# Fourteen scan states fed by TensorE diagonals, scan outputs added by accumulating transposes, filled phase ends and split values in a four-layer kernel

## The chip, the cores and the metric

The kernel runs on one core of one Trainium2 chip. The metric is the device time of one launch in microseconds (us). Each engine has a queue of instructions of its own and waits for others on semaphores: TensorE (PE) multiplies and transposes, VectorE (DVE), ScalarE (ACT) and GpSimd (POOL) work on elements, SyncE (SP) issues transfers.

## The reference

x has 1024 tokens (4 sequences of 256) of 512 values, all fp32. Four layers follow, each between two norms:

```
x = x + ln(ssm(ln(x)))          # D_IN 1024, 16 states
x = x + ln(int_ffn(ln(x)))      # 1376 hidden, integer weights, scales per row
x = x + ln(attention(ln(x)))    # 32 query heads, 8 key/value heads, causal
x = x + ln(diff_ffn(ln(x)))     # 1792 hidden
# ssm: dt, B, C from x; for each channel d and state n, over time:
state = state * exp(dt * A) + dt * u * B ;  y = sum_n(state * C) ;  y = (y + x*D) * silu(gate)
# diff_ffn weights: base + mean(|w - base|) * sign(w - base)
```

## The kernel before

The program is a row of phases, each a block in which every engine has its own written-out order: `in` (projection), prologue, `scan`, `fa` (finish), `mi` (widen), `fb`, key and value, attention, `fd`. Nothing schedules at run time but semaphores; a phase's instructions don't start before the phase ahead has ended on all engines. Precise products split both operands in a high and a low part in fp32r: high*high, high*low and low*high, three matmuls. ACT makes the high part, DVE or POOL the low one.

**Scan** (`scan_phase`, L680). A tile is 128 channels of one sequence: 32 tiles, two to a turn of a loop (r = 0, 1). Its 16 states stand as 8 pairs of 2 x 256 columns. Of a pair the decay exp(dt*A) comes from ACT (L861); the inflow dt*u*B comes from POOL for 8 states (L798) and from PE for the other 8, as fp32 matmuls with a diagonal matrix that holds B (L1045, two for a pair). DVE scans each pair (L952, L958). The outputs are weighed with C by DVE for 8 states (L968) and by POOL for 8 (L810). PE adds the 16 weighed states and x*D into y by 17 fp32 matmuls of 256 columns with the identity (L1051, L1077). An fp32 matmul leaves two records in the trace. Two transposes a tile (L1036) turn dt*u for ACT, which makes the diagonals.

**Finish** (`finish_phase`, L160) multiplies the gated y, or the hidden values, with the down weights for 8 tiles of 128 tokens, normalizes, adds to x, normalizes again and transposes the result (L227) into the operands xh, xl of the next phase. **Widen** (`widen_phase`, L460) goes through F steps; a step is 48 matmuls of 512 columns (L538): 2 halves of the weights, 4 blocks of depth, 3 products, 2 halves of the tokens (h). For `mi` it also loads w and base of the last layer (L516), POOL subtracts them (L622) and ACT sums |w - base| (L563), which waits for nobody else in the step. Weights of step f are split by ACT (`prepare`, L558) and DVE (L634). Key and value (L1207) have the same form with steps of half the width.

**Attention** (`attention_mlp_phase`, L1317) makes 32 steps (8 groups g of 4 heads, 4 sequences b). In a step PE does the output products of the step behind it (24 matmuls, L1462 to L1464), transposes the probabilities (L1471, L1476), multiplies them with the values by 3 fp32 matmuls of 512 columns (`attend`, L1480 to L1484), the scores of the next step (L1448, L1450) and its queries (48 matmuls of 256 columns, L1437). DVE takes the maxima (L1817), scales the probabilities (L1828); POOL makes the low parts of the group's weights, wql (L1728) and wol (L1732), and the sine part of the rotation (L1724).

## Time and profile before

The median of 3 runs is 1802.15 us (1801.33 to 1806.17). The profiled execution took 1799.71 us; its span, from the first to the last instruction recorded, is 1797.9 us at a mean granted clock of 0.976.

| engine | busy us | share of the span | instructions |
|---|---|---|---|
| PE (matmuls, transposes) | 1671.7 | 93% | 8214 |
| PEld (weight loads, beside PE) | 1374.2 | 76% | 8214 |
| DVE | 1101.3 | 61% | 1608 |
| ACT | 867.7 | 48% | 1773 |
| POOL | 812.4 | 45% | 414 |

Busy time is an average over phases with different limits, so it is read by phase: the views of windows give it for a stretch, the timeline gives the start of each group of like instructions. A timeline's second column reaches to the modelled end of the last one and overlaps the next; a pace is read from one start to the next start.

### The profile page before, as it was taken

To read this page: it belongs to the slowest core of one execution; us is meant where nothing else is said; L and a number is where in the kernel's file an instruction comes from. 1 tells how busy PE (TensorE), PEld (TensorE's weight loads), DVE (VectorE), ACT (ScalarE), POOL (GpSimd) and SP (SyncE) were. 2 spreads that over 40 slices of the span, in tenths; PEclk is the share of its full clock that TensorE was granted. 3 is DMA by queue.
4 is the path that set the end of the run, shared out by engine and by line. 5 is a ranking of instruction groups with operands and counts; after the bars stand their busy time and mean duration, and the time that the engine had idled before them with its cause. 6 is when DMAs were issued, how large, how long until landed. Compare 5 with 4: busy or idle time off the path is not lost. (4 is left out here: it accounts for less than half of the span.)

```text
span 1797.9 us, 24221 instructions
## 1 busy us (share of the span) xinstructions
PE 1671.7 (93%) x8214; PEld 1374.2 (76%) x8214; DVE 1101.3 (61%) x1608; ACT 867.7 (48%) x1773; POOL 812.4 (45%) x414
## 2 busy tenths in 40 slices
PE   5995999999998799997998999999999999899998
PEld 4862788888886588786876888788787878788877
DVE  4337999999995433352915566665656667755422
ACT  2337777777763354233624454545444445543321
POOL 2212999999994373142612232222322225456333
PEclk9998999999999899998998999999999999899999
DMA  3203010101102393001200000100010010234100
GB/s 115 65 1 120 1 47 24 47 23 34 36 0 94 114 336 146 18 1 44 79 24 24 24 24 24 47 23 23 24 46 23 23 59 36 71 141 147 64 18 30
DMA packets 25188, 100.84 MB, mean 56 GB/s; under 512 B 3104, under 2 KB 3360, under 8 KB 22560
## 3 DMA queue, kind: packets, MB, share of 16 engines
q1 hardware_dynamic: 24976, 99.89, 15.6%
q8 instruction: 40, 0.66, 0.1%
q14 instruction: 28, 0.23, 0.0%
q10 hardware_dynamic: 144, 0.07, 0.0%
HBM read 97.72 MB, written 2.23 MB: 56 GB/s over the span
## 5 line engine op out<-in xcount | busy, mean ns | idle before, releaser
L1051 PE MATMUL psum<-scratch_s,res_const 128*128 128x256 f32 x1024 | 250.3, 382 | 4.3 <-DVE scratch_s L968 3.6
L1724 POOL TENSOR_TENSOR stretch_turned<-stretch_turned,res_const 128x1024 f32<-128x1024 f32 x32 | 79.4, 2481 | 359.5 <-ACT stretch_turned L1574 359.5
L1051 PEld LDWEIGHTS psum<-scratch_s,res_const 128*128 128x128 f32 x1024 | 191.7, 190 | 42.6 <-DVE scratch_s L968 17.9
L810 POOL TENSOR_TENSOR scratch_s<-scratch_s,scan_cm 128x1024 f32<-128x1024 f32 x64 | 151.0, 2359 | 32.1 <-DVE scratch_s L952 32.1
L1437 PE MATMUL psum<-opnd_xh,query_wqh 128*128 128x256 f32 x512 | 149.9, 293 | 8.9 <-POOL query_wql L1728 6.3
L952 DVE TENSOR_TENSOR_SCAN scratch_s<-psum,scratch_s 128x512 f32<-128x512 f32 x128 | 153.3, 1197 | 7.7 <-ACT psum L861 7.7
L798 POOL TENSOR_TENSOR scratch_s<-scan_bm,scratch_s 128x1024 f32<-128x1024 f32 x64 | 151.0, 2361 | 0.1
L1437 PE MATMUL psum<-opnd_xh,query_wql 128*128 128x256 f32 x512 | 144.8, 283 | 0.0
L1437 PE MATMUL psum<-opnd_xl,query_wqh 128*128 128x256 f32 x512 | 144.8, 283 | 0.0
L1045 PE MATMUL psum<-scan_diag,scratch_s 128*128 128x256 f32 x512 | 133.2, 384 | 6.6 <-ACT scratch_s L853 6.6
L1582 ACT ACTIVATE stretch_pa<-psum,stretch_nm 128x128 f32<-128x128 f32 x128 | 45.4, 366 | 178.2 <-DVE stretch_nm L1817 178.2
L861 ACT ACTIVATE psum<-ssm_dt,ssm_vec 128x255 f32 (+1 forms) x256 | 110.8, 464 | 11.5 <-DVE scratch_s L952 11.0
L1045 PEld LDWEIGHTS psum<-scan_diag,scratch_s 128*128 128x128 f32 x512 | 96.1, 193 | 19.3 <-issue 7.2
L1437 PEld LDWEIGHTS psum<-opnd_xh,query_wqh 128*128 128x128 f32 x512 | 98.2, 192 | 12.6 <-issue 11.9
L1462 PE MATMUL psum<-stretch_woh,stretch_oh 128*128 128x512 f32 x256 | 100.3, 392 | 0.5 <-DVE stretch_ol L1925 0.5
L1463 PE MATMUL psum<-stretch_wol,stretch_oh 128*128 128x512 f32 x256 | 100.0, 391 | 0.0
L1464 PE MATMUL psum<-stretch_woh,stretch_ol 128*128 128x512 f32 x256 | 99.9, 390 | 0.0
L1437 PEld LDWEIGHTS psum<-opnd_xl,query_wqh 128*128 128x128 f32 x512 | 98.0, 191 | 0.6
L1437 PEld LDWEIGHTS psum<-opnd_xh,query_wql 128*128 128x128 f32 x512 | 98.0, 191 | 0.0
L968 DVE TENSOR_TENSOR scratch_s<-psum,scan_cm 128x512 f32<-128x512 f32 x128 | 85.1, 665 | 0.0
L958 DVE TENSOR_TENSOR_SCAN psum<-scan_decay,psum 128x512 f32<-128x512 f32 x64 | 78.3, 1224 | 0.0
L958 DVE TENSOR_TENSOR_SCAN psum<-scratch_s,psum 128x512 f32<-128x512 f32 x64 | 78.3, 1223 | 0.0
(298 smaller groups left out, 4296.3 us busy)
## 6 DMA issues: line engine op xcount, KB each, us to landing
mi_dw<-in_dw SPq DMA_DIRECT2D x24, 448.0 KB, 5.8
mi_dm<-in_dm SPq DMA_DIRECT2D x24, 448.0 KB, 6.4
query_raw<-in_w_q SPq DMA_DIRECT2D x8, 1024.0 KB, 4.7
query_raw<-in_w_o SPq DMA_DIRECT2D x8, 1024.0 KB, 4.8
scan_cm<-bc_rows SPq DMA_DIRECT2D x12, 512.0 KB, 4.3
gu_raw<-in_w_gu SPq DMA_DIRECT2D x11, 512.0 KB, 7.7
mlpa_raw<-in_w_mlp SPq DMA_DIRECT2D x7, 768.0 KB, 4.3
mlpa_base<-in_b_mlp SPq DMA_DIRECT2D x7, 768.0 KB, 5.9
```

Source lines behind the costliest of these rows:

```text
L798: nc.gpsimd.tensor_tensor(by_state(shared[r][h]), bm[:, 4 * h:4 * h + 4, :], u[r].rearrange("p (a t) -> p a t", a=1).broadcast_to((P, 4, S ...
L810: nc.gpsimd.tensor_tensor(shared[r][h], shared[r][h], weights(4 * h, 4), ALU.mult).then_inc(weighted_pool, 1)
L861: ins = nc.scalar.activation(by_state(bank)[:, n, 1:SEQ], flat_dt[:, bass.ds(s * SEQ + 1, SEQ - 1)], ACT.Exp, scale=M.vec[:, bass.ds(s * N ...
L952: nc.vector.tensor_tensor_scan(quarter(r, i), decay_shared[i % 2], quarter(r, i), 0.0, ALU.mult, ALU.add).then_inc(scanned, 1)
L958: nc.vector.tensor_tensor_scan(state[i], decay_own[i % 2], state[i], 0.0, ALU.mult, ALU.add).then_inc(scanned, 1)
L968: nc.vector.tensor_tensor(own[i], state[i], weights(NH + 2 * i, 2), ALU.mult).then_inc(weighted, 1)
L1045: mm = nc.tensor.matmul(by_state(state[i])[:, :, t * P:(t + 1) * P], ut[r][:, t * P:(t + 1) * P], diag[:, t, 2 * i:2 * i + 2, :], start=Tr ...
L1051: mm = nc.tensor.matmul(ps_y[r], ident, part[:, n * SEQ:(n + 1) * SEQ], start=False, stop=stop and (n + 1) * SEQ == part.shape[1])
L1437: mm = nc.tensor.matmul(ps_q[:, h * SEQ:(h + 1) * SEQ], w[:, k, h * HD:(h + 1) * HD], x[:, k, b * SEQ:(b + 1) * SEQ], start=(k == 0 and w ...
L1462: nc.tensor.matmul(X[t], oh[:, t, part], woh[:, h, :], start=(h == 0), stop=False)
L1463: nc.tensor.matmul(X[t], oh[:, t, part], wol[:, h, :], start=False, stop=False)
L1464: mm = nc.tensor.matmul(X[t], ol[:, t, part], woh[:, h, :], start=False, stop=(h == HPG - 1))
```

## The change

**Scan.** PE makes the inflow of 14 of the 16 states (7 pairs), POOL that of 2. The states of the 7 pairs stand in five PSUM banks by the tables BANK and DECAY. DVE still scans all 8 pairs, five of them straight into SBUF slots that POOL weighs; DVE weighs two. The outputs are added by transposes of 128 x 128 that accumulate in PSUM (34 a tile), and the sum is transposed back (2 a tile). ACT makes the diagonals of the next sequence spread over the tiles, where before it made them at the change of sequence.

The order on PE for one tile of the scan, before (scratch_s holds the weighed states, res_const the identity, scan_diag the diagonals):

```order
L1045 MATMUL psum<-scan_diag,scratch_s 128x2x128 x2
L1051 MATMUL psum<-scratch_s,res_const 128x256 x2
L1045 MATMUL psum<-scan_diag,scratch_s 128x2x128 x2
L1051 MATMUL psum<-scratch_s,res_const 128x256 x6
L1045 MATMUL psum<-scan_diag,scratch_s 128x2x128 x2
L1051 MATMUL psum<-scratch_s,res_const 128x256 x2
L1045 MATMUL psum<-scan_diag,scratch_s 128x2x128 x2
L1051 MATMUL psum<-scratch_s,res_const 128x256 x4
L1077 MATMUL psum<-scratch_s,res_const 128x256
L1051 MATMUL psum<-scratch_s,res_const 128x256 x2
L1036 MATMUL psum<-res_const,scratch_s 128x128 x2
```

Eight inflow matmuls, 17 additions of 256 columns, two transposes. After, one tile:

```order
L1129 MATMUL psum<-res_const,scratch_s 128x128 x4
L1123 MATMUL psum<-scan_diag,scratch_s 128x2x128 x2
L1129 MATMUL psum<-res_const,scratch_s 128x128 x8
L1110 MATMUL psum<-res_const,scratch_s 128x128 x2
L1123 MATMUL psum<-scan_diag,scratch_s 128x2x128 x2
L1129 MATMUL psum<-res_const,scratch_s 128x128 x2
L1155 MATMUL psum<-res_const,scratch_s 128x128 x2
L1123 MATMUL psum<-scan_diag,scratch_s 128x2x128 x2
L1129 MATMUL psum<-res_const,scratch_s 128x128 x12
L1123 MATMUL psum<-scan_diag,scratch_s 128x2x128 x4
L1129 MATMUL psum<-res_const,scratch_s 128x128 x8
L1123 MATMUL psum<-scan_diag,scratch_s 128x2x128 x4
```

L1123 is now 14 matmuls, L1129 (34) adds, L1110 (2) flips dt*u and L1155 (2) brings the sum back.

**Phase ends.** While `fa` and `fb` run, the first weights of the next phase are split (2 steps of `mi`, 3 of key and value), and PE multiplies them with the first half of the tokens (`next_product`, 12 matmuls each: 4 for `mi`, 3 for key and value), two of them among the last transposes, the others behind them. The next phase then does only the second half (h = 1) of these steps. SP loads the weights of step f + 2 earlier. In `mi` ACT no longer does `prepare` of steps 0 and 1, and does the silu of a step ahead of the sums of |w - base|.

ACT at the start of `mi`, before (mi_wh: high parts of weights; mi_dw: the differences; mi_mid: the silu):

```order
L558 ACTIVATE mi_wh_6112<-gu_raw_73 128x1024
L558 ACTIVATE mi_wh_6113<-gu_raw_74 128x1024
L563 ACTIVATE mi_dw_6118,res_diff_sums<-mi_dw_6118 128x896 x3
L595 ACTIVATE mi_mid_6116<-psum,gu_gate_s 128x1024
L558 ACTIVATE mi_wh_6112<-gu_raw_73 128x1024
L563 ACTIVATE mi_dw_6121,res_diff_sums<-mi_dw_6121 128x896 x3
L595 ACTIVATE mi_mid_6117<-psum,gu_gate_s 128x1024
```

And after:

```order
L627 ACTIVATE mi_mid_7493<-psum,gu_gate_s 128x1024
L595 ACTIVATE mi_dw_7495,res_diff_sums<-mi_dw_7495 128x896 x3
L590 ACTIVATE mi_w_wh_6749<-gu_raw_76 128x1024
L627 ACTIVATE mi_mid_7494<-psum,gu_gate_s 128x1024
L595 ACTIVATE mi_dw_7498,res_diff_sums<-mi_dw_7498 128x896 x3
L590 ACTIVATE mi_w_wh_6750<-gu_raw_77 128x1024
```

The first high part that `mi` still has to make (L590, for step 2) stands behind silu(0) and the three sums of step 0; before, the first two stood ahead of everything.

**Attention.** Values and probabilities are split (V by ACT and POOL, P by ACT and DVE) and `attend` is 9 fp32r matmuls. The probabilities are transposed into the banks of the scores, ahead of the last 6 of the 24 output matmuls. The low parts wql and wol are made in two pieces by heads; POOL begins wol only when the second maxima of the group are there (`neg_max`). In between, copies of values and of turned probabilities go.

PE from the last output products to the scores of step 1, before (stretch_pt: turned probabilities, stretch_vs: values):

```order
L1462 MATMUL psum<-stretch_woh,stretch_oh 128x512
L1463 MATMUL psum<-stretch_wol,stretch_oh 128x512
L1464 MATMUL psum<-stretch_woh,stretch_ol 128x512
L1471 MATMUL psum<-res_const,stretch_pa 128x128 x4
L1476 MATMUL psum<-res_const,stretch_pb 128x128 x8
L1480 MATMUL psum<-stretch_pt,stretch_vs 128x512
L1482 MATMUL psum<-stretch_pt,stretch_vs 128x512
L1484 MATMUL psum<-stretch_pt,stretch_vs 128x512
L1448 MATMUL psum<-att_k,stretch_q 128x128 x4
L1450 MATMUL psum<-att_k,stretch_q 128x256 x4
```

And after, in the same place (stretch_ph, _pl and stretch_vh, _vl: high and low parts):

```order
L1586 MATMUL psum<-res_const,stretch_pa 128x128 x4
L1590 MATMUL psum<-res_const,stretch_pb 128x128 x8
L1576 MATMUL psum<-stretch_woh,stretch_oh 128x512
L1577 MATMUL psum<-stretch_wol,stretch_oh 128x512
L1578 MATMUL psum<-stretch_woh,stretch_ol 128x512
L1576 MATMUL psum<-stretch_woh,stretch_oh 128x512
L1577 MATMUL psum<-stretch_wol,stretch_oh 128x512
L1578 MATMUL psum<-stretch_woh,stretch_ol 128x512
L1602 MATMUL psum<-stretch_ph,stretch_vh 128x512
L1603 MATMUL psum<-stretch_ph,stretch_vl 128x512
L1602 MATMUL psum<-stretch_ph,stretch_vh 128x512
L1603 MATMUL psum<-stretch_ph,stretch_vl 128x512
```

Six output matmuls now stand behind the transposes. The last two rows shown repeat once more; three matmuls of stretch_pl with stretch_vh follow, and then the scores.

The diff, cut to what the prediction speaks of:

```diff
+            def next_product(i):
+                bank, split, hi, lo = next_products[i]
+                pe.wait_ge(next_hi, split + 1)
+                pe.wait_ge(next_lo, split + 1)
+                at_least(pe, x_lo, TT // 2)
+                for k in range(KM):
+                    for j, (w, x) in enumerate(((hi, M.xh), (hi, M.xl), (lo, M.xh))):
+                        nc.tensor.matmul(M.ps[:, bank, :], w(k), x[:, k, 0:HALF], start=(k == 0 and j == 0),
+                                         stop=(k == KM - 1 and j == 2))
...
+                if next_products and TT <= t < TT + 2:
+                    next_product(t - TT)
...
+            for i in range(2, len(next_products)):
+                next_product(i)
...
+                if 0 <= t - 2 < len(next_split):
+                    raw, hi, _ = next_split[t - 2]
+                    act.wait_ge(next_in, 16 * len(next_split))
+                    nc.scalar.activation(hi, raw, ACT.Copy).then_inc(next_hi, 1)
...
+                elif exists(f + 2, F):
+                    at_least(sp, w_lo, f + 1 - done)
+                    sp.dma_start(raw[s][:, :], raw_dram[:, cols(f + 2, RC)]).then_inc(raw_in[s], 16)
...
+                first = 1 if isinstance(f, int) and f < done else 0
                 for a in range(2):
                     for k in range(KM):
                         for w, x in ((wh, M.xh), (wh, M.xl), (wl, M.xh)):
-                            for h in range(2):
+                            for h in range(first, 2):
...
-                if exists(f + 1, F):
+                if exists(f + 1, F) and not (isinstance(f, int) and f + 1 < done):
                     prepare(f + 1, 1 - s)
-                if diff is not None and exists(f, N_SUMS):
+                if diff is not None and exists(f, N_SUMS) and done == 0:
...
+                    if diff is not None and done:
+                        if exists(f, N_SUMS):
+                            differences(f, s)
...
+    NC, PAIRS, SLOTS, OWN = 2, 7, 3, 2
+    NT = NC * PAIRS
+    OWN_AT = (1, 4)
+    BANK, DECAY = (0, 1, 2, 3, 0, 4, 2, 3, 1, 4, 0, 3, 2, 4), (0, 1, 2, 0, 1, 2, 0, 1, 2, 3, 0, 1, 2, 3)
...
+                pool.wait_ge(scanned, scans_by(s, (0, 3, 6)[h]))
+                nc.gpsimd.tensor_tensor(slot[h][r], slot[h][r], weights(4 * h, 4), ALU.mult).then_inc(weighted_pool, 1)
...
+                    decay_pair(s, r, 3)
+                    decay_pair(s, r, 4)
                     if not first:
-                        finish(s - 1, 1 - r)
+                        keep(s - 1)
                     if not last:
                         turn(s + 1, 1 - r)
+                    decay_pair(s, r, 5)
+                    decay_pair(s, r, 6)
+                    if not first:
+                        finish(s - 1)
+                    if not last:
+                        decay_start(s + 1)
                         skip(s + 1, 1 - r)
-                    if renew:
-                        diagonals(s, 1, b + 1)
+                    if b < BATCH - 1:
+                        diagonals(b + 1, j * 2 + r)
...
+            def recur(s, r, p):
+                dve.wait_ge(inflow_pe, s * PAIRS + p + 1)
+                dve.wait_ge(decayed, s * PAIRS + p + 1)
+                out = state_of(r, p)
+                if p in slot_of:
+                    h = slot_of[p] // 2
+                    at_least(dve, summed_pool, (s - (2 if h == 0 else 1)) * SLOTS + h + 1)
+                    out = half_slot(r, slot_of[p])
+                nc.vector.tensor_tensor_scan(out, decay_of(r, p), state_of(r, p), 0.0, ALU.mult, ALU.add).then_inc(scanned, 1)
...
+                    recur_first(s, r)
+                    for p in range(PAIRS):
+                        if p - 1 in OWN_AT:
+                            weigh_ready(s, OWN_AT.index(p - 1), b)
+                        recur(s, r, p)
+                        if p - 1 in OWN_AT:
+                            weigh(s, r, OWN_AT.index(p - 1))
...
+            def add(part, start=False, stop=False):
+                for t in range(QT):
+                    mm = nc.tensor.matmul(ps_y[:, t * P:(t + 1) * P], part[:, t * P:(t + 1) * P], ident,
+                                          start=start and t == 0, stop=stop and t == QT - 1, is_transpose=True)
                 return mm
...
+                    inflow(s, r, 3, b)
+                    if not first:
+                        own_sums(s - 1, 1)
+                    inflow(s, r, 4, b)
+                    if not first:
+                        slot_sums(s - 1, 1 - r, 2)
+                    if not last:
+                        flip(s + 1, 1 - r)
+                    inflow(s, r, 5, b)
+                    begin(s, r)
+                    if not first:
+                        back(s - 1)
+                    inflow(s, r, 6, b)
+                    slot_sums(s, r, 0)
+                    own_sums(s, 0)
+                    if not last:
+                        inflow(s + 1, 1 - r, 0, nb)
+                        inflow(s + 1, 1 - r, 1, nb)
+                    slot_sums(s, r, 1)
+                    if not last:
+                        inflow(s + 1, 1 - r, 2, nb)
...
+                early = HPG if ending(g, b, BATCH - 1) else HPG // 2
+                if any_behind:
+                    output(*behind, 0)
+                    output(*behind, 1, 0, early)
+                flips(g, b)
+                if any_behind and early < HPG:
+                    output(*behind, 1, early)
                 attend(g, b)
...
+                for i, (bank, keys) in enumerate(((X[2], 0), (X[0], 0), (X[0], 1))):
+                    pe.wait_ge(p_hi, v * 3 + i + 1)
+                    if i == 1:
+                        at_least(pe, added, v * 2 - 1)
+                    nc.tensor.matmul(bank, vh[:, keys, :], ph[:, i, :], start=(i < 2), stop=False)
+                    nc.tensor.matmul(bank, vl[:, keys, :], ph[:, i, :], start=False, stop=False)
+                pe.wait_ge(p_lo, v * 3 + 1)
+                nc.tensor.matmul(X[2], vh[:, 0, :], pl[:, 0, :], start=False, stop=True).then_inc(summed, 1)
+                pe.wait_ge(p_lo, v * 3 + 3)
+                nc.tensor.matmul(X[0], vh[:, 0, :], pl[:, 1, :], start=False, stop=False)
+                nc.tensor.matmul(X[0], vh[:, 1, :], pl[:, 2, :], start=False, stop=True).then_inc(summed, 1)
...
+                pool.wait_ge(neg_max, g * BATCH + 2)
+                for h in (slice(0, 2), slice(2, HPG)):
+                    nc.gpsimd.tensor_tensor(wol[:, h, :], raw[:, :].rearrange("p (h c) -> p h c", h=HPG)[:, h, :],
+                                            f32(woh[:, h, :]), ALU.subtract).then_inc(wo_lo, 1)
...
+                for i in range(3):
+                    dve.wait_ge(p_hi, v * 3 + i + 1)
+                    nc.vector.tensor_tensor(pl[:, i, :], turned_p[i], f32(ph[:, i, :]), ALU.subtract).then_inc(p_lo, 1)
```

## Rows read from the trace of the kernel before

**Rows 1.** Windows, scan then attention: stretch, length; busy PE, PEld, DVE, ACT, POOL; clock; DMA; GB/s.

```profile
180.00:540.00 360.00, 353.44 (x1624) 298.61 (x1624) 355.51 (x379) 260.21 (x644) 334.19 (x186) 1.00 0.08 27
936.00:1500.00 564.00, 542.99 (x3201) 454.86 (x3202) 348.51 (x659) 264.46 (x677) 148.90 (x47) 0.99 0.09 31
```

**Rows 2.** The page: span; 40 slices of PE busy and granted clock.

```profile
span 1797.9 us, 24221 instructions
PE   5995999999998799997998999999999999899998
PEclk9998999999999899998998999999999999899999
```

**Rows 3.** Timeline of DVE in the scan: start, length, engine, line, operation.

```profile
269.38 0.67 DVE L968 TENSOR_TENSOR scratch_s<-psum,scan_cm 128x512 f32<-128x512 f32 x1
269.96 1.22 DVE L958 TENSOR_TENSOR_SCAN psum<-scratch_s,psum 128x512 f32<-128x512 f32 x1
...
272.21 0.67 DVE L968 TENSOR_TENSOR scratch_s<-psum,scan_cm 128x512 f32<-128x512 f32 x1
```

**Rows 4.** Timeline of PE in the scan.

```profile
401.71 1.03 PE L1045 MATMUL psum<-scan_diag,scratch_s 128*128 128x256 f32 x4
402.57 1.03 PE L1051 MATMUL psum<-scratch_s,res_const 128*128 128x256 f32 x4
```

**Rows 5.** Timeline of POOL in the scan.

```profile
272.37 2.36 POOL L810 TENSOR_TENSOR scratch_s<-scratch_s,scan_cm 128x1024 f32<-128x1024 f32 x1 [1.78 <-DVE scratch_s L952]
```

**Rows 6.** Timeline of PE after the two-step sums widened: products at full clock.

```profile
641.32 0.62 PE L538 MATMUL psum<-opnd_xh,mi_wl 128*128 128x512 f32 x2
641.77 0.62 PE L538 MATMUL psum<-opnd_xh,mi_wh 128*128 128x512 f32 x2
```

**Rows 7.** Timeline of PE at 1111 us: transposes and what follows.

```profile
1111.31 0.60 PE L1471 MATMUL psum<-res_const,stretch_pa 128*128 128x128 f32 x4
1111.75 1.17 PE L1476 MATMUL psum<-res_const,stretch_pb 128*128 128x128 f32 x8
1112.75 1.02 PE L1480 MATMUL psum<-stretch_pt,stretch_vs 128*128 128x512 f32 x2
1115.33 1.05 PE L1448 MATMUL psum<-att_k,stretch_q 128*128 x8
```

**Rows 8.** Timeline from fa into mi, all engines.

```profile
611.72 1.11 PE L227 MATMUL psum<-res_const,stretch_xn 128*128 128x128 f32 x4 [3.56 <-ACT stretch_xn L284]
615.04 0.33 SPq L516 DMA_DIRECT2D mi_dw<-in_dw  x1
617.52 1.19 PE L538 MATMUL psum<-opnd_xh,mi_wh 128*128 128x512 f32 x2 [4.69 <-DVE mi_wl L634]
624.60 6.28 POOL L622 TENSOR_TENSOR mi_dw<-mi_dw,mi_dm 128x896 f32<-128x896 f32 x3 [14.04 <-DMA mi_dm<-in_dm]
630.92 0.95 ACT L563 ACTIVATE mi_dw<-mi_dw 128x896 f32<-128x896 f32 x1 [1.05 <-POOL mi_dw L622]
635.71 3.05 DVE L634 TENSOR_TENSOR mi_wl<-gu_raw,mi_wh 128x1024 fp32r<-128x1024 int32 x1
```

**Rows 9.** Timeline of PE in the key and value phase: steps 0 and 3.

```profile
824.11 1.19 PE L1207 MATMUL psum<-opnd_xh,kv_wh 128*128 128x512 f32 x2 [1.28 <-POOL kv_wl L1268]
842.08 0.61 PE L1207 MATMUL psum<-opnd_xh,kv_wh 128*128 128x512 f32 x2
```

**Rows 10.** Waits of 940 to 1530 us: engine, tile <- releaser: us, times, longest.

```profile
PE psum L1437 <- POOL query_wql L1728: 6.3, 6, 1.0
```

**Rows 11.** Timeline of DVE and POOL in attention.

```profile
1108.20 1.13 DVE L1828 TENSOR_SCALAR stretch_pb<-stretch_pb,stretch_inv 128x256 f32<-128x256 f32 x4
1118.00 4.62 POOL L1732 TENSOR_TENSOR stretch_wol<-query_raw,stretch_woh 128x2048 fp32r<-128x2048 f32 x1 [6.20 <-ACT stretch_woh L1597]
1121.33 1.31 DVE L1817 TENSOR_SCALAR stretch_nm<-stretch_mx 128x8 f32<-128x8 f32 x1
```

**Rows 12.** Timeline of PE at the scan's start, low clock.

```profile
174.85 4.79 PE L1045 MATMUL psum<-scan_diag,scratch_s 128*128 128x256 f32 x12 [6.62 <-ACT scratch_s L853]
```

More of the change, by code:

```diff
@@ L460, in widen_phase @@
 def widen_phase(nc, tag, M, place, F, kind, raw_dram, base_dram=None, hidden=None,
-                x_conv=None, gate=None, scales=None, coeff=None, second=None, diff=None, raw=None, base=None, ahead=(), next_w=None):
+                x_conv=None, gate=None, scales=None, coeff=None, second=None, diff=None, raw=None, base=None, ahead=(), next_w=None, begun=None):
     signals = Signals(nc)
@@ L644, in step @@
             def step(f, s):
-                if kind == "int" and exists(f + 1, F):
+                if kind == "int" and exists(f + 1, F) and not (isinstance(f, int) and f + 1 < done):
                     int_lows(f + 1, 1 - s)
@@ L857, in skip, with decays @@
                                      scale=M.vec[:, bass.ds(s + V_D, 1)]).then_inc(skip_ready, 1)
-            def decays(s, bank, first):
+            def decays(s, bank, first, signal):
                 for n in range(NC):
@@ new lines, in begin, with slot_sums, own_sums @@
+            def begin(s, r):
+                pe.wait_ge(skip_ready, s + 1)
+                at_least(pe, y_copied, s)
+                add(xd[r], start=True)
+            def slot_sums(s, r, h):
+                pe.wait_ge(weighted_pool, s * SLOTS + h + 1)
+                for n in range(2 * NC):
+                    mm = add(slot[h][r][:, n * SEQ:(n + 1) * SEQ], stop=h == SLOTS - 1 and n == 2 * NC - 1)
+                mm.then_inc(summed_pool, 1)
+            def own_sums(s, i):
+                pe.wait_ge(weighted, s * OWN + i + 1)
+                for n in range(NC):
+                    mm = add(own[i][:, n * SEQ:(n + 1) * SEQ])
+                mm.then_inc(summed, 1)
@@ L1114, in _, with key_value_phase @@
             pe.wait_ge(dt_done, KI)
+            inflow(0, 0, 2, 0)
             pairs(pe, body)
-            shared_sums(TILES - 1, 1, 1)
+            own_sums(TILES - 1, 1)
+            slot_sums(TILES - 1, 1, 2)
+            back(TILES - 1)
     signals.close()
-def key_value_phase(nc, M, place, spare, raw, K, V, ch, cl, w_kv, w_v, wq_raw, wqh, wql, wq):
+def key_value_phase(nc, M, place, spare, raw, wh, wl, K, V, ch, cl, w_kv, w_v, wq_raw, wqh, wql, wq):
     signals = Signals(nc)
@@ L1669, in body @@
                     act.wait_ge(summed, v * 2 + t + 1)
-                    nc.scalar.activation(oh[:, t, :], x, ACT.Copy).then_inc(o_hi, 1)
+                    nc.scalar.activation(oh[t], x, ACT.Copy).then_inc(o_hi, 1)
                     if ending(g, b, BATCH - 1) and t == 0:
                         y_norm(2)
+                if more(g, b):
+                    values_high(*after(g, b))
                 if b == 0:
@@ L1680, in _ @@
             turn(0, 0)
+            values_high(0, 0)
             exps(0, 0)
@@ L1761, in body @@
                     query_weights(g + 1)
+                if more(g, b):
+                    values_low(*after(g, b))
                 if b == 0:
```

519 lines of the change are left out of this document (271 added, 248 removed).

## The prediction

> **What bounds the kernel now.** I read the windows first. In the scan, PE is busy for 353.4 of 360 us and DVE for 355.5, POOL for 334.2 and ACT for 260.2 [rows 1]: two engines are full and a third nearly. In attention PE alone is, with 543.0 of 564 us, and no other engine reaches 350 [rows 1]. The page's slices show PE at 9 tenths nearly everywhere, with holes in slices 1, 4, 14 and 22 above all [rows 2]; slice 14 (584 to 629 us) holds the end of `fa`. Then I read the timeline of each stretch for its pace and for who lets whom go on.
>
> In the scan a DVE round is two scans (2.25 us, 1.125 each) and a weighing (.58), and starts every 2.83 us [rows 3]. A tile is four rounds, 11.32 us; 32 tiles are 362 us, and with the 4.5 us that DVE lacks in the window [rows 1] the scan lasts 366.7. PE's tile is nearly as long: four records, which are two fp32 matmuls of 256 columns, take .86 us [rows 4], so a matmul .43 and 25 of them 10.75, with two transposes at .11 (four take .44 [rows 7]) 10.97. To relieve one engine alone would gain under .4 us a tile; the change relieves both.
>
> **The scan, part by part.** DVE keeps eight scans and has two weighings fewer: 8 x 1.125 + 2 x .58 = 10.16 us a tile. PE gets six inflow matmuls more, 14 x .43 = 6.02, and drops the 17 additions for 34 transposes, with four others 38 x .11 = 4.18; together 10.20. Twelve transposes in a row take 1.44 us, .12 each [rows 7], which would make it 10.58. POOL today spends 334.2 x 11.32/360 = 10.51 us a tile, four of its operations being 1024 columns at 2.36 [rows 5]; the 1.07 left stays, and 3 x 2.36 + 1.18 (its one inflow pair) makes 9.33. ACT has 260.2 x 11.32/360 = 8.18, and six diagonals' more work and one more copy leave it below 10. So three engines lie within 1.3 us of each other at 10.2 to 10.6. I take 10.4: 333 us instead of 366.7. The diagonals are made over the tiles and not at the change of sequence, which takes the 4.5 us away; of the 33.7 gained I leave 1.7 to the first and last tile: **-32**. The best that these rows allow is DVE's own 10.16, 325 us, -41. The other bound: PE at 10.58 and one wait of half a microsecond a tile, since five banks and six slots go round between DVE, PE and POOL: 11.08 x 32 = 355, -12.
>
> **fa into mi.** Before, PE starts `mi` at 617.52, and its 97th matmul at 641.77 [rows 6, 8]; 24.25 us, where 96 at .225 (two in .45 [rows 6]) are 21.6; the rest, 2.6, goes to the low clock at the start. Now the last transposes (611.72 [rows 8]) have 24 of the 48 early products behind them: .44 + 24 x .225 brings PE to 617.6, the phase change (estimate 1.0) to 618.6, and the 48 matmuls left of steps 0 and 1 to 629.5. Step 2 needs `prepare(2)`, which ACT has behind silu(0) and the three sums of |w - base|. Those wait for transfers and POOL: from the issue of w to POOL's start it was 615.04 to 624.60, 9.56 us, and POOL took 6.28 [rows 8]. The issues now start at about 619.9, behind raw(2) on SP; so POOL runs 629.5 to 635.8, ACT's last sum ends 1.2 later as before (630.92 + .95 against 630.88 [rows 8]), 637.0; the high part takes 1.1 (1024 columns by the .95 for 896), the low one on DVE 3.05 [rows 8]. Step 2 starts at 641.2, .6 earlier, after 11.7 us without PE, and then pays the low clock's 2.6 a second time: **+2**. Silu(0), kept from waiting, gains nothing since the step after is late. Bounds: with early differences, 629.5 for 641.8, -12; with the transfers 3 us slower, as w and its base then compete with raw(3), +5.
>
> **fb into key and value.** Before, step 0 starts at 824.11 and step 3 at 842.08 [rows 9]. No sums stand in the way here. Of 36 early products 12 are behind the last transposes, 2.7 us, where PE had waited for weights anyway (1.28 at 824.11 [rows 9]). Steps 0 to 2 then have 36 matmuls, 8.1 us at .225, and no cold start: step 3 at 832.1. **-10**, between -12 and -7 (if the products start behind the phase's waits, not in them).
>
> **Attention.** `attend` was three fp32 matmuls of 512 columns: 1112.75 to 1115.33 [rows 7], 2.58 us. Nine at .225 are 2.03: -.55 x 32 = -17. In two pieces wql is there when the first heads start: its 6.3 us [rows 10] go, and with what hangs on them I count -8. Against this, wol: POOL started it at 1118.00 and needed 4.62; now it waits for the maxima, which end between 1121.33 and 1122.64 [rows 11] (8 columns can hardly need 1.31 us; POOL was running then, and that is the wait this order removes). Taking .55 off for the shorter `attend`, the halves are ready at 1123.1 and 1125.4, or 1.2 later; PE comes to the outputs 6 us of queries and 2.3 of scores after 1114.8, at 1123.1, and to the third head 1.37 later. The second half is .9 to 2.2 us late, in 8 steps; 1.25 each, +10. The probabilities were ready at 1109.33 (1108.20 + 1.13 [rows 11]) for transposes at 1111.31 [rows 7], 1.98 us of slack, and six output products (1.36) move from ahead of them to behind: .6 is left, enough on average; what it costs if it is not is up to 4. DVE's three low parts are at work while PE does the six. Together **-15**, between -25 (no late wol) and -3 (both waits).
>
> **Sum.** -32 + 2 - 10 - 15 = -55. The profiled execution took 1799.7, so 1744.7; the median of the runs is 2.45 above it: **1747**.
>
> **What speaks against it.** At the start of the scan twelve fp32 records took 4.79 us [rows 12], .40 each where .215 is the pace of [rows 4]: the granted clock is then at 1.2 GHz instead of 2.4, after 6.62 us without work. In slice 4 PE was busy 5 tenths and was granted 8 tenths of the clock; in the scan, with .98 busy, it had 1.00 [rows 1, 2], but only two transposes a tile are in that, so the scan before doesn't show what 38 do. In attention 12 of a step's are in a row without a fall. The Trainium skill ("TensorE: Matmul & The Clock Gate", Part 4: PE-mode transpose) says that a transpose doesn't count as PE being busy in the way a matmul does, and that the full clock doesn't engage for it; by that rule the clock could fall in the scan, by the 12 in attention that run at full pace it doesn't.
>
> **Rivals.**
> A. The clock falls in the scan (slower). Matmuls make up 6.02 of PE's 10.4 us a tile, .58, about the share of slice 4. At its .8, a tile is 10.4/.8 = 13.0 us, the scan 416, +49 instead of -32: 1828. At the low level throughout, 28 records x .40 and 38 x .22 are 19.6 us a tile, 627: about 2040. It decides from a mean clock of .855 in the scan on, since there 10.4/.855 x 32 = 389 eats the 23 us won elsewhere. For it: slice 4. Against: the run of 12, and that no ten microseconds of the scan are free of matmuls. Chance .07.
> B. The rings stall: .5 to .9 us a tile of DVE waiting for a bank that PE has not filled, because PE does 38 additions in the order of the program and one that waits for POOL holds up the next inflow. For: POOL at 9.33 of 10.4 has little room. Against: before its 1024 columns POOL waited 1.78 us for DVE [rows 5], so today's ring has room to spare. That takes 16 to 29 off the 32: 1763 to 1776. Chance .17.
> C. The differences of `mi` don't hold ACT up, since the transfers land sooner: -12 instead of +2, 1733. For: 9.56 us is long for three transfers, and SP had others ahead of them. Chance .13.
> D. The transposes are slower than those of before when they add to PSUM (.16 or more each): PE at 12.1 a tile, the scan 20 us longer than before: 1799, no change. Nothing in the trace adds by a transpose. Chance .04.
> The forecast as it stands: .59.
>
> **Range and chances.** 8 times in 10 the time should lie from 1728 (C with the scan's better bound in part) to 1790; this leaves out A, D, and the sum of all lower bounds. A measurement of this kernel can tell about .3%, 5.4 us, from no change. Faster .89, within it .03, slower .08.
>
> **What the profile after would show.** In the scan a tile every 10.3 to 10.6 us on DVE with a clock of 1.00; a period above 11 with waits of DVE for PE is B, a clock under .95 is A. In `mi`, PE idle for about 11.7 us before step 2, behind ACT's sums; if this is under 3 us, C. Step 3 of key and value 8 us after step 0, not 18. Attention steps of 17.3 us, no wait for wql, and eight waits of about 1.2 us for wol. I am wrong if the scan is not the largest part of the gain.

## The result

The changed kernel takes 1750.26 us (median of 5 runs, 1749.63 to 1751.48) against 1802.15: the ratio is 0.9708, with a 95% interval of 0.9693 to 0.9724. Forecast were 1747 and a range of 1728 to 1790. The profiled execution took 1750.26 us with a span of 1748.5. So the total came out within 3.3 us, but not its terms: the scan gave 40 us and not 32, attention 4 and not 15.

The changed kernel by windows (stretch, length, busy time of PE, PEld, DVE, ACT and POOL, granted clock, DMA share, GB/s), to be held against [rows 1]:

```profile
180.00:500.00 320.00, 320.00 (x2065) 289.46 (x2064) 319.26 (x316) 269.52 (x711) 300.33 (x186) 1.00 0.09 29
936.00:1500.00 564.00, 538.48 (x3297) 477.22 (x3296) 412.34 (x738) 287.81 (x751) 181.15 (x101) 0.99 0.10 35
```

In the scan PE and DVE are both full, POOL and ACT are closer to it than before, and the clock is 1.00. In attention DVE is busy for 412 us where it was for 349; part of that is time in which its instructions stand still, as shown below.

Where the time went is read from the first or last instruction of each phase. The timeline of PE before: first product of `fa`, first query, last transposes of attention.

```profile
553.72 0.76 PE L251 MATMUL psum<-stretch_wh,stretch_hh 128*128 128x512 f32 x1 [6.61 <-ACT stretch_wh L303]
...
936.64 0.35 PE L1437 MATMUL psum<-opnd_xh,query_wqh 128*128 128x256 f32 x1 [1.92 <-PEq L94]
...
1532.36 1.12 PE L1471 MATMUL psum<-res_const,stretch_pa 128*128 128x128 f32 x4 [4.56 <-DVE stretch_pb L1828]
```

And after: first product of `fa`, first and third step of `mi`, step 0 and 3 of key and value, first query, last transposes.

```profile
513.97 0.76 PE L262 MATMUL psum<-stretch_wh,stretch_hh 128*128 128x512 f32 x1 [6.62 <-ACT stretch_wh L322]
...
581.66 0.47 PE L570 MATMUL psum<-opnd_xh,mi_w_wh 128*128 128x512 f32 x1 [0.90 <-PEq L94]
...
603.39 1.19 PE L570 MATMUL psum<-opnd_xh,mi_w_wh 128*128 128x512 f32 x2 [10.59 <-issue]
...
788.21 0.48 PE L1312 MATMUL psum<-opnd_xh,kv_w_wh 128*128 128x512 f32 x1
...
796.48 0.62 PE L1312 MATMUL psum<-opnd_xh,kv_w_wh 128*128 128x512 f32 x2
...
891.03 0.36 PE L1547 MATMUL psum<-opnd_xh,query_wqh 128*128 128x256 f32 x1 [1.91 <-PEq L94]
...
1482.76 1.12 PE L1586 MATMUL psum<-res_const,stretch_pa 128*128 128x128 f32 x4 [5.29 <-DVE stretch_pb L1977]
```

| stretch | forecast | measured | from |
|---|---|---|---|
| scan | -32 | -40.2 | 553.72 to 513.97, started .43 later |
| `fa` and `mi` | +2 | +5.1 | last product of `mi` at 739.24, now 704.61 |
| `fb` | 0 | -1.3 | 824.11 [rows 9], now 788.21 |
| key and value | -10 | -9.7 | 936.64, now 891.03 |
| attention | -15 | -4.0 | 1532.36, now 1482.76 |
| last layer | 0 | +.2 | span 1797.9, now 1748.5 |

**Scan.** The timeline of DVE after (start, us, engine, line): the first scan of the first tile, a weighing and the same one a tile later, the first scan of the last tile.

```profile
177.45 1.22 DVE L1025 TENSOR_TENSOR_SCAN scratch_s<-psum,scratch_s 128x512 f32<-128x512 f32 x1 [3.26 <-ACT psum L919]
...
256.46 0.67 DVE L1043 TENSOR_TENSOR scratch_s<-psum,scan_cm 128x512 f32<-128x512 f32 x1
...
266.55 0.67 DVE L1043 TENSOR_TENSOR scratch_s<-psum,scan_cm 128x512 f32<-128x512 f32 x1
...
492.52 1.20 DVE L1025 TENSOR_TENSOR_SCAN scratch_s<-psum,scratch_s 128x512 f32<-128x512 f32 x1
```

10.09 us a tile here, 10.16 over the 31 tiles from 177.45 to 492.52. PE in the same tile, additions and inflow:

```profile
255.47 1.47 PE L1129 MATMUL psum<-res_const,scratch_s 128*128 128x128 f32 x12
256.78 1.89 PE L1123 MATMUL psum<-diag_odd_diag,scratch_s 128*128 128x256 f32 x8
258.51 1.04 PE L1129 MATMUL psum<-res_const,scratch_s 128*128 128x128 f32 x8
```

Twelve accumulating transposes take 1.31 us, .109 each, the pace of the plain ones [rows 7]; eight fp32 records 1.73.

**Attention.** From one step's transposes to the next it was 17.86, 18.66, 19.14 and 17.87 us in a group of four steps; it is 19.75, 17.33, 17.48 and 17.25. So I had taken three of four steps right (17.3 was forecast) and missed the first, and the last three of the whole phase: 23.26, 18.91 and 18.87 where they were 17.94, 18.54 and 16.91. The waits of PE in attention after (us, times, longest) name two releasers:

```profile
PE psum L1586 <- DVE stretch_pb L1977: 18.5, 10, 5.3
PE psum L1576 <- POOL stretch_wol L1873: 7.2, 14, 0.7
```

and the timelines of DVE and POOL in a group's long step show DVE's scaling instructions growing when POOL works:

```profile
1073.44 0.17 DVE L1966 TENSOR_SCALAR stretch_nm<-stretch_mx 128x8 f32<-128x8 f32 x1
1077.38 1.78 DVE L1975 TENSOR_SCALAR stretch_pa<-stretch_pa,stretch_inv 128x128 f32<-128x128 f32 x4
1079.08 3.28 DVE L1977 TENSOR_SCALAR stretch_pb<-stretch_pb,stretch_inv 128x256 f32<-128x256 f32 x4
...
1073.76 4.73 POOL L1873 TENSOR_TENSOR stretch_wol<-query_raw,stretch_woh 128x1024 fp32r<-128x1024 f32 x2 [4.26 <-DVE stretch_nm L1966]
1079.26 2.43 POOL L1861 TENSOR_TENSOR stretch_turned<-stretch_turned,res_const 128x1024 f32<-128x1024 f32 x1 [0.77 <-ACT stretch_turned L1704]
```

```profile
917.06 0.87 DVE L1975 TENSOR_SCALAR stretch_pa<-stretch_pa,stretch_inv 128x128 f32<-128x128 f32 x4
917.85 1.14 DVE L1977 TENSOR_SCALAR stretch_pb<-stretch_pb,stretch_inv 128x256 f32<-128x256 f32 x4
```

The second fence has the same two lines in the first step, where POOL is idle: .87 and 1.14 us for four instructions each. In the long step the four of L1975 take 1.78 and are done only after wol has ended (1078.49), and those of L1977 hang from the start of the sine product (1079.26) and are done .7 us after its end (1081.69): 3.28 us for the four. The negative maxima (L1966), which took 1.31 us before beside wol [rows 11], take .17 now: the wait moved POOL's work from ahead of a small instruction to ahead of eight larger ones. PE in the same step waits for both halves of wol and then for the scaled probabilities:

```profile
1076.39 0.47 PE L1576 MATMUL psum<-stretch_woh,stretch_ph 128*128 128x512 f32 x1 [0.43 <-POOL stretch_wol L1873]
...
1078.54 0.51 PE L1576 MATMUL psum<-stretch_woh,stretch_ph 128*128 128x512 f32 x1 [0.54 <-POOL stretch_wol L1873]
...
1082.42 0.66 PE L1586 MATMUL psum<-res_const,stretch_pa 128*128 128x128 f32 x4 [0.82 <-DVE stretch_pb L1977]
```

In the last group POOL does wol (from 1433.11), the subtraction of mlp weights and the sine product (to 1443.59) without a pause. The four of L1975 hang beside all three, and PE waits 4.04 us for the scaling before the transposes of 1444.98:

```profile
1436.30 7.58 DVE L1975 TENSOR_SCALAR stretch_pa<-stretch_pa,stretch_inv 128x128 f32<-128x128 f32 x4
```

### The profile page after: what moved, and what is told of

Read it like the earlier page. It is cut to its first block and busy times, and to the rows that moved or that the text cites. A ratio compares the mean times of both kernels' runs of the same rounds, so it can differ in the third digit from the quotient of the medians.

```text
span 1748.5 us, 25644 instructions
## 1 busy us (share of the span) xinstructions
PE 1618.7 (93%) x8758; PEld 1379.1 (79%) x8758; DVE 1118.6 (64%) x1580; ACT 895.7 (51%) x1905; POOL 802.8 (46%) x458
## 5 line engine op out<-in xcount | busy, mean ns | idle before, releaser
L863 POOL TENSOR_TENSOR scratch_s<-scratch_s,scan_cm 128x1024 f32<-128x1024 f32 x96 | 227.4, 2369 | 25.5 <-DVE scratch_s L1035 25.4
L1129 PE MATMUL psum<-res_const,scratch_s 128*128 128x128 f32 x1088 | 144.7, 273 | 2.2 <-POOL scratch_s L863 2.2
L1129 PEld LDWEIGHTS psum<-res_const,scratch_s 128*128 128x128 f32 x1088 | 128.7, 141 | 18.3 <-POOL scratch_s L863 2.4
L919 ACT ACTIVATE scratch_s<-ssm_dt,ssm_vec 128x255 f32 (+1 forms) x256 | 112.4, 500 | 11.0 <-DVE scratch_s L1035 8.4
L1123 PE MATMUL psum<-scan_diag,scratch_s 128*128 128x256 f32 x448 | 111.8, 385 | 6.7 <-ACT scratch_s L911 6.7
L1123 PE MATMUL psum<-diag_odd_diag,scratch_s 128*128 128x256 f32 x448 | 110.0, 380 | 0.0
L1035 DVE TENSOR_TENSOR_SCAN scratch_s<-scratch_s,psum 128x512 f32<-128x512 f32 x80 | 96.6, 1208 | 0.5 <-ACT scratch_s L919 0.2
L1035 DVE TENSOR_TENSOR_SCAN scratch_s<-decays_decay,psum 128x512 f32<-128x512 f32 x80 | 96.1, 1201 | 0.3
L1123 PEld LDWEIGHTS psum<-scan_diag,scratch_s 128*128 128x128 f32 x448 | 80.5, 194 | 15.2 <-issue 7.0
L1123 PEld LDWEIGHTS psum<-diag_odd_diag,scratch_s 128*128 128x128 f32 x448 | 79.0, 191 | 7.3
L919 ACT ACTIVATE decays_decay<-ssm_dt,ssm_vec 128x255 f32 (+1 forms) x192 | 83.1, 502 | 0.0
L660 POOL TENSOR_TENSOR mi_dw<-mi_dw,mi_dm 128x896 f32<-128x896 f32 x24 | 54.0, 2276 | 50.4 <-DMA mi_dm<-in_dm 50.4
```

What stands on the lines that cost most here:

```text
L660: nc.gpsimd.tensor_tensor(dw[s][:, a, :], dw[s][:, a, :], dm[s][:, a, :], ALU.subtract).then_inc(d_sub, 1)
L863: nc.gpsimd.tensor_tensor(slot[h][r], slot[h][r], weights(4 * h, 4), ALU.mult).then_inc(weighted_pool, 1)
L919: ins = nc.scalar.activation(by_state(bank)[:, n, 1:SEQ], flat_dt[:, bass.ds(s * SEQ + 1, SEQ - 1)], ACT.Exp, scale=M.vec[:, bass.ds(s * N ...
L1035: nc.vector.tensor_tensor_scan(out, decay_of(r, p), state_of(r, p), 0.0, ALU.mult, ALU.add).then_inc(scanned, 1)
L1123: mm = nc.tensor.matmul(by_state(state_of(r, p))[:, :, t * P:(t + 1) * P], ut[r][:, t * P:(t + 1) * P], diag[b % 2][:, t, NC * PLACE[p]:NC ...
L1129: mm = nc.tensor.matmul(ps_y[:, t * P:(t + 1) * P], part[:, t * P:(t + 1) * P], ident, start=start and t == 0, stop=stop and t == QT - 1, ...
```

## The experiments

Each is the changed kernel with the edit shown. Times are medians, ratios are to the kernel before.

### The first half of wol ahead of the maxima

```diff
-                pool.wait_ge(neg_max, g * BATCH + 2)
                 for h in (slice(0, 2), slice(2, HPG)):
+                    if h.start:
+                        pool.wait_ge(neg_max, g * BATCH + 2)
```

> POOL no longer waits for the maxima before the first half of wol, only before the second. Theory M (DVE's scaling of the probabilities stands still while POOL subtracts or multiplies): the first half runs in the 3.4 us before the maxima are there, the second is over before the scaling starts; of the 2.5 us that the step after a group's first has over the others (19.75 against 17.25) 2 or more go, in 8 groups, and up to 4 in the last group: 1750 becomes 1728 to 1734. Rival L (only the late wol costs, .43 + .54 us a group): 1742.

1730.74 us, ratio 0.9601 (0.9584 to 0.9619). The long step is 17.24 in every group; the last three are 20.79, 18.75 and 18.85. POOL and DVE in this kernel, in the same step:

```profile
1068.12 2.40 POOL L1874 TENSOR_TENSOR stretch_wol<-query_raw,stretch_woh 128x1024 fp32r<-128x1024 f32 x1 [0.94 <-ACT stretch_woh L1732]
1071.36 2.40 POOL L1874 TENSOR_TENSOR stretch_wol<-query_raw,stretch_woh 128x1024 fp32r<-128x1024 f32 x1 [0.84 <-DVE stretch_nm L1967]
1076.93 2.42 POOL L1861 TENSOR_TENSOR stretch_turned<-stretch_turned,res_const 128x1024 f32<-128x1024 f32 x1 [3.17 <-ACT stretch_turned L1704]
...
1075.04 0.88 DVE L1976 TENSOR_SCALAR stretch_pa<-stretch_pa,stretch_inv 128x128 f32<-128x128 f32 x4
1075.83 1.14 DVE L1978 TENSOR_SCALAR stretch_pb<-stretch_pb,stretch_inv 128x256 f32<-128x256 f32 x4
```

One half ends before the maxima are there, the other before the scaling starts, and the scaling has its short times again. Theory L, by which only the .97 us of late wol counts, would have given 1742 and is out. But this edit removes the late halves together with the long scaling, so it doesn't say how the 2.5 us divide; the edit of the sine product below does.

### No wait for the maxima

```diff
-                pool.wait_ge(neg_max, g * BATCH + 2)
```

> Neither half of wol waits for the maxima. Theory M: POOL's 4.7 us then cover the little instruction that makes the negative maxima (some 1.5 us later than now), but not the scaling; the long step becomes 17.8 to 18.2, and the last group's 23.3 falls by 5: 1728 to 1736. Rival L (only the late wol costs): 1742, with no lengthening of the negative maxima.

1735.48 us, ratio 0.9638 (0.9618 to 0.9658). The long step is 18.30, a little above the 17.8 to 18.2 expected, the last three 18.24, 17.51 and 18.87. The negative maxima stand beside POOL's 4.75 us (1066.71 to 1071.46) and end with it:

```profile
1066.71 4.75 POOL L1872 TENSOR_TENSOR stretch_wol<-query_raw,stretch_woh 128x1024 fp32r<-128x1024 f32 x2 [0.94 <-ACT stretch_woh L1732]
...
1069.70 1.79 DVE L1965 TENSOR_SCALAR stretch_nm<-stretch_mx 128x8 f32<-128x8 f32 x1
```

So the wait in the change is right in what it protects, and too long by one half.

### The sine product behind the scaling

```diff
                 if more(g, b):
+                    pool.wait_ge(normed, g * BATCH + b + 1)
                     sine(*after(g, b))
```

> POOL's sine product waits until DVE has scaled the probabilities; wol stays as it is. Theory M: in the long step the scaling is freed of the second of its two disturbers and ends at about 1080.5 instead of 1082.4, ahead of PE, so .98 us a group goes: 1742 (1740 to 1744). Rival: the scaling is slow for another reason (its operands, the semaphores), then 1750 or slower, since the sine comes later.

1740.18 us, ratio 0.9663 (0.9644 to 0.9681). The long step is 18.76, .99 less, as forecast. Of the two instructions of POOL that held up the scaling only wol is left: L1976 is long, L1978 short. PE no longer waits for the scaling here (it is done at 1077.91, the transposes start at 1079.14), so the 1.51 us that are left over 17.25 go with its two waits for wol, .42 and .54 as before. Of the 2.50 us, then, 1.0 are the scaling and 1.5 the late wol.

```profile
1075.08 1.78 DVE L1976 TENSOR_SCALAR stretch_pa<-stretch_pa,stretch_inv 128x128 f32<-128x128 f32 x4
1076.78 1.13 DVE L1978 TENSOR_SCALAR stretch_pb<-stretch_pb,stretch_inv 128x256 f32<-128x256 f32 x4
```

The last group gains too (23.26 and 18.91 become 20.85 and 17.29), which I had not expected: the sine product, 2.4 us, is one of the three that its scaling hung beside. With it the sum is some 10 us.

### The sums of `mi` one step later

```diff
-                        if exists(f, N_SUMS):
-                            differences(f, s)
+                        if not (isinstance(f, int) and not 1 <= f <= N_SUMS):
+                            differences(f - 1, 1 - s)
```

> In mi, ACT makes the three sums of a step one step later, behind the next step's high parts and silu. Theory A (ACT's queue: the high part of step 2 stands behind sums that wait 8.4 us for transfers and POOL): PE's hole of 10.6 us goes, and the low clock after it: -11 to -13, 1737 to 1739. Rival T (the transfers are what is late, the raw weights of step 2 too): the hole stays or moves by one step, 1748 to 1752.

1734.45 us, ratio 0.9627 (0.961 to 0.9644). `mi` starts at 581.55 and its last product at 690.0, not 704.61. ACT in the changed kernel, and then in this one:

```profile
594.21 0.95 ACT L595 ACTIVATE mi_dw<-mi_dw 128x896 f32<-128x896 f32 x1 [8.40 <-POOL mi_dw L660]
...
599.22 1.04 ACT L590 ACTIVATE mi_w_wh<-gu_raw 128x1024 fp32r<-128x1024 int32 x1
```

```profile
587.36 1.07 ACT L590 ACTIVATE mi_w_wh<-gu_raw 128x1024 fp32r<-128x1024 int32 x1 [1.67 <-PE psum L570]
...
594.26 0.95 ACT L595 ACTIVATE mi_dw<-mi_dw 128x896 f32<-128x896 f32 x1 [3.13 <-POOL mi_dw L660]
```

The sums come when they came; the high part is 11.9 us earlier, PE's hole is gone, and with it the slow start behind it: 14.6 us. The transfers were not late for the weights.

### `mi` as before

Leaves out `next_split` and `next_products` of `fa` and sets `done = 0` in `mi`.

> fa ends and mi starts as in the kernel before (no weights split in fa, no early products, high parts ahead of the sums); key and value keeps its early products. The traces say that from the first product of fa to the end of mi the changed kernel is 5.1 us longer. Theory A (the early products don't pay while the sums stand ahead of the high part): 1745 (1743 to 1747). Rival: the 5.1 us come from the order of SP and from the transfers in mi, or from the scan's end, and the early products themselves pay: 1750 or more.

1743.53 us, ratio 0.9682 (0.9657 to 0.9707), 6.7 less than the changed kernel. From the first product of `fa` to its last transposes it is 57.9 us (58.0 before, 60.7 in the changed kernel). `mi` starts at 577.29 instead of 581.66 and ends at 698.49 instead of 704.61. The early products of `fa`, with the splitting in `fa` and the later place of the high parts that came with them, cost time as they were built in, and with the sums out of the way (the experiment above) they are worth 8.5 us against this one.

### The additions as matmuls

```diff
-    start=start and t == 0, stop=stop and t == QT - 1, is_transpose=True)
+    start=start and t == 0, stop=stop and t == QT - 1)
```

> The 34 additions of a scan tile are the same instructions without the transpose flag, so fp32 matmuls of 128 columns with two records each. Theory P (PE's pace per addition carries the scan's gain): PE's tile is 14 x .433 + 34 x .215 + 4 x .11 = 13.8 us in place of 10.1, and the scan 118 us longer: 1868. Rival R (the gain comes from the five banks and from DVE's two weighings fewer, and PE has room): the tile stays under 11.5 us, 1795 at most.

1872.79 us, ratio 1.0395 (1.0372 to 1.0417). First scan of the first and of the last tile:

```profile
178.10 1.22 DVE L1025 TENSOR_TENSOR_SCAN scratch_s<-psum,scratch_s 128x512 f32<-128x512 f32 x1 [3.26 <-ACT psum L919]
...
609.48 1.20 DVE L1025 TENSOR_TENSOR_SCAN scratch_s<-psum,scratch_s 128x512 f32<-128x512 f32 x1
```

(609.48 - 178.10)/31 is 13.92 us a tile, 2.6 more than before the change (11.32 by [rows 3]). With the additions as matmuls the five banks and DVE's fewer weighings would have been a loss; it is the transposes that pay. Theory R is out.

### Fewer additions

```diff
-                for n in range(2 * NC):
+                for n in range(2 * NC if h != 1 else 1):
```

> Leaves 6 of the 34 additions out in every tile of the scan (y lacks three of the states' pairs' parts): PE has .65 us less in a tile of 10.09. Theory D (DVE alone sets the tile now): 1750, the tile stays 10.09. Rival E (PE sets it, since its 14 x .433 + 38 x .109 = 10.2 leaves it no idle time in the windows): the tile falls to 9.5 or to what DVE allows, up to -19.

1748.57 us, ratio 0.9703 (0.9685 to 0.9721). DVE's first scan stands at 177.45 as in the changed kernel; that of the last tile:

```profile
490.19 1.20 DVE L1025 TENSOR_TENSOR_SCAN scratch_s<-psum,scratch_s 128x512 f32<-128x512 f32 x1
```

10.09 us in every tile, where the changed kernel has 10.16 on average: 10.09 in its first nine, and then 10.08 to 10.37, PE's own 10.19. So D is right, but for .07 us a tile, which is E's: DVE's own tile is 10.09.

### Narrow own weighings

```diff
-    nc.vector.tensor_tensor(own[i], state_of(r, OWN_AT[i]), weights(...), ALU.mult)
+    nc.vector.tensor_tensor(own[i][:, 0:P], state_of(r, OWN_AT[i])[:, 0:P], weights(...)[:, 0:P], ALU.mult)
```

> Leaves out three quarters of DVE's two weighings and the 6 additions of these parts in a tile (y lacks them): DVE's tile becomes about 9.3 us, PE's 9.5. Theory D and E alike: the tile falls to 9.5, -18: 1732. Rival F (POOL, whose three weighings, one inflow and small products are 9.5 us with the waits between them, or the ring of banks is next): 9.9 or more, -6 at most, with waits of DVE or PE for POOL.

1730.39 us, ratio 0.9602 (0.9584 to 0.9621).

```profile
177.43 1.22 DVE L1025 TENSOR_TENSOR_SCAN scratch_s<-psum,scratch_s 128x512 f32<-128x512 f32 x1 [3.26 <-ACT psum L919]
...
473.15 1.20 DVE L1025 TENSOR_TENSOR_SCAN scratch_s<-psum,scratch_s 128x512 f32<-128x512 f32 x1
```

```profile
180.00:480.00 300.00, 299.88 (x1877) 266.90 (x1876) 294.97 (x315) 268.57 (x710) 298.56 (x186) 1.00 0.09 31
```

9.54 us a tile, with PE at 299.9 and POOL at 298.6 of 300 us and DVE at 295.0. The gain is as forecast, and rival F stands right behind it: three engines end within two per cent of each other.

### The fixes together

The sums one step later, the first half of wol early (in the last group both halves), with and without the sine's wait.

> The changed kernel with the sums of mi one step later, the first half of wol ahead of the maxima (in the last group both halves) and the sine product behind the scaling. If the effects add: 1750 less 16 (sums) less 19.5 (first half of wol) less 4 (last group) is 1711 (1708 to 1715). Rival: what one edit frees the other had already freed, or the sine's wait costs in the last group, 1716 or more.

> As the combined kernel, without the sine product's wait. Where the first half of wol is early, the sine product overlaps only the end of the scaling, and PE comes to the transposes later than that: within 1.5 us of the combined kernel. Rival: the sine still delays the scaling past PE's arrival, then 3 us or more above it.

1711.06 us, ratio 0.9489 (0.9473 to 0.9505), and 1709.17 us, ratio 0.9479 (0.9464 to 0.9495). The effects add: 1711 was the sum. Without the sine's wait it is no slower, as the overlap has gone with wol. The last three steps are 18.25, 17.5 and 18.89.

### The last step

In the last step one more of DVE's lines was long beside POOL, in the changed kernel:

```profile
1475.40 4.03 DVE L2030 SCALAR_TENSOR_TENSOR down_down<-mlpa_raw,res_coeff,mlpa_base 128x512 f32<-128x512 f32 x1
...
1475.41 3.48 POOL L1894 TENSOR_TENSOR mlpb_raw<-mlpb_raw,mlpb_base 128x1536 f32<-128x1536 f32 x1
```

Both edits put a wait ahead of POOL's subtraction, on top of the combined kernel without the sine's wait:

```diff
                     mlp_low(0)
+                    pool.wait_ge(mw_down, 1)      # the first of the two
+                    pool.wait_ge(normed, U)       # in its place, the second
                     difference(1)
```

> As the combined kernel without the sine's wait; in the last step of attention POOL's second subtraction of mlp weights (3.48 us) waits until DVE has made the down weights. Now DVE's scalar_tensor_tensor of two SBUF operands takes 4.03 us beside POOL's 3.48, in the kernel before it took .74. Theory M: it takes .74 again and the last step, 18.9 us, becomes 17.7 to 18.1; a gain of about 1 us in all. Rival: the instruction is slow for its own operands' sake, the step stays 18.9.

> The same, but POOL's subtraction waits until DVE has scaled the probabilities too. Theory M: the last step becomes 17.1 to 17.5; the sign of the differences on ACT then comes 5 us later, and if the first steps of the last layer have no room for that, the time goes back: between 1.6 us faster and 4 us slower than without the wait.

```profile
1435.20 0.74 DVE L2032 SCALAR_TENSOR_TENSOR down_down<-mlpa_raw,res_coeff,mlpa_base 128x512 f32<-128x512 f32 x1
...
1436.02 3.45 POOL L1895 TENSOR_TENSOR mlpb_raw<-mlpb_raw,mlpb_base 128x1536 f32<-128x1536 f32 x1 [0.77 <-DVE down_down L2032]
```

1708.74 us, ratio 0.9479 (0.9464 to 0.9494), and 1712.94 us, ratio 0.9496 (0.948 to 0.9512). The line takes .74 again and the last step 17.56, with the second wait 17.23. The totals cannot tell the first from 1709.17. The second is 3.8 us slower, near the worst that was expected: ACT's sign of the differences now waits 5.75 us for POOL and stands ahead of its high parts of the probabilities, so from the last transposes to the first product with the values PE takes 5.61 us where the first has 2.48.

## Why the forecast was right in the sum and wrong in its terms

**Scan, -32 forecast, -40.2 measured.** The mechanism held: two full engines, both relieved. What was mis-sized is the tile: I worked out DVE 10.16 and PE 10.20 to 10.58, took 10.4 and gave 1.7 us to the ends. What came is 10.16 as the mean, the low bound that was named with -41. It isn't quite DVE's own: that is 10.09, and PE's 10.19 makes the rest. The .12 from twelve transposes in attention was the wrong row: after the change, with other matmuls behind them, the same twelve take 1.23 us (1421.72 to 1422.95). The .11 from four was right.

Of the rivals, B (rings that stall) would have shown waits of DVE for PE; the view of waits has none in the scan, and what its 31 tiles have over 10.09 is 2.3 us in all. D asked for .16 us a transpose; it is .109.

**The clock.** Granted 1.00 through the scan, with 38 transposes in every 10.1 us. By the rule of the Trainium skill ("TensorE: Matmul & The Clock Gate", Part 4: PE-mode transpose) that a transpose doesn't hold the clock up, rival A would have given 1828 or more; this trace doesn't bear it out for 38 transposes beside 14 fp32 matmuls in a tile. A scan of transposes alone was not run.

**`fa` into `mi`, +2 forecast, +5.1 measured.** The step that named the sums was right: the hole was 10.59 us for a forecast 11.7, and taking the cause away gave 14.6 back. Rival C's gain exists, but by an order on ACT and not by earlier transfers: from the issue of w at 582.00 to POOL's start at 592.09 it is 10.1 us, and was 9.56. Wrong was that the last transposes of `fa` start when they did. They start at 574.63 where 611.72 less 39.75 is 571.97, and `mi` starts 2.8 us later than I had it. The early products are not what delays them: the transposes two tiles earlier, at 567.49, already come 2.66 us late (before: 604.58), and the first early product starts only at 567.84. The time is lost before, in the steps of `fa` that also split the next weights. ACT's two high parts there (1.05 us each) stand ahead of the high part of the gated y, DVE's low parts stand ahead of its norms, and one of them, 1.22 us when free, takes 2.82 beside POOL; holes of PE of .96, 1.32 and 1.45 us appear where two of .31 were.

```profile
552.31 2.82 DVE L451 TENSOR_TENSOR mi_w_wl<-gu_raw,mi_w_wh 128x1024 fp32r<-128x1024 int32 x1
...
561.92 0.47 PE L262 MATMUL psum<-stretch_wh,stretch_hh 128*128 128x512 f32 x1 [1.45 <-issue]
...
567.49 0.60 PE L238 MATMUL psum<-res_const,stretch_xn 128*128 128x128 f32 x4
```

Without splitting and early products `fa` has its old length again (`mi` as before, above); the two were not taken out one by one. The prediction had no term for the splitting in `fa`. Another 1.2 us are lost behind step 2: from there to the end of `mi` it is 101.2 us where it was 97.5, 3.8 more for the 2.6 forecast.

**Key and value, -10, measured -9.7.** Step 3 comes 8.3 us after step 0 (788.21 to 796.48), where it was 18.0.

**Attention, -15 forecast, -4.0 measured.** The gain in `attend` is there (nine matmuls in 2.06 us, steps of 17.25), and so are the late halves of wol, with waits of .43 and .54 us. Together they cost 1.5 us a group, as the experiment with the sine product shows, for the 1.25 forecast: this term was right. The step that failed is the one that took the slack between the scaled probabilities and the transposes as "enough on average". It was worked out for a step in which POOL is idle. The prediction itself said that POOL's running stretched the negative maxima to 1.31 us, and moved POOL's 4.62 us back by some 4 us without asking what DVE does there: the scaling. That costs 1.0 us in the first step of seven groups, some 7 in all. In the last group, where two more instructions of POOL follow wol at once, PE waits 4.0 us for the scaling in the first step, and the three steps together are 7.7 us longer than before. Against this, attention without these holds gained some 5 us more than the 25 counted for it.

The rest is 1.7 us at the start of attention. The first 48 queries take 7.5 us instead of 6.0: from 892.5 to 895.9 they go at .21 each and not .12, and the granted clock of the first ten microseconds is .83 where it was 1.00, though PE had stood idle for 1.9 us ahead of them both times. From the first query to the first transposes it is 28.0 us here, 26.3 before, and 26.3 again in the combined kernel, so this is not put down to the change; what decides it stays open.

One reading of the page was incomplete: slice 19, the start of key and value, is as low (7 tenths) as slice 14 and lower than slice 22. No term rests on it.

The two errors, 8 and 11 us, stand against each other. The 3.3 us between forecast and result are luck as much as working. Between the two spans the change gave 49.4 us and not 55; the 2.45 us that were added for the median, which the run after does not need, hide some of it.

## What to carry to other kernels

When work is moved in time or to another engine, follow the moved instruction to its new neighbours: what one engine's long elementwise instruction blocks on another is decided by when it runs, so a wait that protects one small instruction can be paid by eight others; ask for the smallest piece that has to wait. When two engines are full, a change pays only as far as the fuller of the two goes; here the plain sum of its durations, without a margin, was right to .1 us in a tile of 10. A sum over phases can be right with two wrong terms, so check each phase against the trace before believing the model.

## What the runs showed of the hardware

DVE's instructions that scale SBUF data by a value per partition stand still while POOL's elementwise instruction on SBUF runs: 8 columns took 1.79 us in place of .17, four of 256 columns 3.28 in place of 1.14, four of 128 columns 7.58 in place of .87 beside three instructions of POOL in a row, and scalar_tensor_tensor with two SBUF operands 4.03 in place of .74. DVE's reductions from PSUM did not slow down: the larger maxima took 1.21 us beside wol in the kernel before, and 1.21 beside an idle POOL after.

```profile
1120.09 1.21 DVE L1815 TENSOR_REDUCE stretch_mx<-psum 128x4 f32<-128x1024 f32 x1
```

```profile
1072.19 1.21 DVE L1964 TENSOR_REDUCE stretch_mx<-psum 128x4 f32<-128x1024 f32 x1
```

The Trainium skill ("SBUF — State Buffer", section "SBUF: two separate sides") says that DVE and GpSimd share one pair of ports under an exclusive lock, which an instruction holds to its end; these times agree, and the order of POOL's work decides who waits.

Transposes that accumulate in PSUM cost .109 us for 128 columns, fp32, the same as plain ones, where the same addition as an fp32 matmul costs .22.
